# Expert layer's end: gathers after the last tile but one, the last tile's rows by one-hot products

## What is computed

```python
x = _layernorm(x)                                   # 1024 tokens, 512 wide
top1 = argmax(softmax(x @ w_router + b_router))     # one of 8 experts for each token
for e in range(8):
    h = gelu(x @ w1[e] + b1[e])                     # 512 -> 2048
    y = h @ w2[e] + b2[e]                           # 2048 -> 512
    out = out + where(top1 == e, y, 0)
x = x + out
```

## Time and profile before

| | us |
|---|---|
| median of three runs | 1984.2 (1982.53 to 1984.51) |
| the profiled execution | 1984.76 |
| its span | 1982.9 |
| busy: TensorE products | 1884.8 (95%) |
| busy: VectorE, ScalarE, GpSimd | 1132.3, 781.4, 803.7 |

### The profile page before, as it was taken

How to read it: one execution, slowest core, us unless ns; L and a number is a source line. 1 busy time by engine, 2 the same in 40 slices (tenths; PEclk the granted TensorE clock), 3 DMA queues, 4 the chain that set the end, 5 groups by cost and what they waited for, 6 DMA issues and landing times. The chain is left out here.

```text
span 1982.9 us, 41168 instructions
## 1 busy us (share of the span) xinstructions
PE 1884.8 (95%) x17350; PEld 1443.9 (73%) x17350; DVE 1132.3 (57%) x2155; ACT 781.4 (39%) x1300; POOL 803.7 (41%) x641
## 2 busy tenths in 40 slices
PE   7999999999999999999999999779879999999995
PEld 6777777777777677677677676657657787989995
DVE  4536556656556557556556666845665353445554
ACT  3224343444444344344334333531234240455663
POOL 2116777677677667677677664000000000100001
PEclk9999999999999999999999999989889999899998
DMA  6122022122122122122121211020031202899993
GB/s 209 54 91 75 28 76 80 33 76 70 41 78 70 39 81 70 39 76 64 50 76 60 65 39 44 30 68 22 2 132 44 91 1 91 343 377 355 356 361 103
DMA packets 107817, 201.28 MB, mean 102 GB/s; under 512 B 9105, under 2 KB 46417, under 8 KB 102529
## 3 DMA queue, kind: packets, MB, share of 16 engines
q1 hardware_dynamic: 106176, 194.44, 28.9%
q0 software_dynamic: 1472, 4.40, 0.7%
HBM read 184.38 MB, written 14.44 MB: 100 GB/s over the span
## 5 line engine op out<-in xcount | busy, mean ns | idle before, releaser
L303 POOL TENSOR_TENSOR arena<-arena,probT 128x512 f32<-128x512 f32 x392 | 502.1, 1281 | 232.0 <-ACT probT L351 207.8
L456 DVE TENSOR_REDUCE negm<-bank 128x1 f32<-128x512 f32 x512 | 327.0, 686 | 181.5 <-PE bank L651 177.1
L437 DVE TENSOR_TENSOR probT<-bank,arena 128x512 f32<-128x512 f32 (+1 forms) x512 | 291.5, 616 | 212.2 <-PE bank L663 212.2
L351 ACT ACTIVATE probT<-probT 128x1024 f32<-128x1024 f32 x256 | 271.1, 1059 | 230.7 <-DVE probT L437 217.8
L345 ACT ACTIVATE arena<-bank 128x512 f32<-128x512 f32 x128 | 76.4, 597 | 474.0 <-PE bank L626 474.0
L279 POOL TENSOR_TENSOR h_lo<-ctx_raw,h_hi 128x512 fp32r<-128x512 f32 x124 | 161.0, 1299 | 172.6 <-ACT h_hi L328 168.0
L681 PEld LDWEIGHTS bank<-probT,arena 128*32 128x32 f32 x4096 | 104.0, 109 | 93.7 <-ACT probT L351 92.3
L626 PE MATMUL bank<-h_hi,w_hi 128*128 128x512 f32 x512 | 152.7, 420 | 11.2 <-ACT h_hi L328 11.2
L663 PEld LDWEIGHTS bank<-q,k 32*128 32x128 f32 x4096 | 126.0, 186 | 46.5 <-issue 44.2
L626 PE MATMUL bank<-w_hi,h_hi 128*128 128x512 f32 x512 | 152.3, 419 | 0.0
L663 PE MATMUL bank<-q,k 32*128 32x128 f32 x4096 | 150.2, 283 | 0.5 <-DVE probT L437 0.5
(11 more groups left out here) (240 smaller groups left out, 2727.3 us busy)
## 6 DMA issues: line engine op xcount, KB each, us to landing
arena<-w SPq DMA_DIRECT2D x10, 4096.0 KB, 14.5
w_sb<-w SPq DMA_DIRECT2D x40, 1024.0 KB, 6.5
x_res<-bias_table SPq DMA_DIRECT2D x64, 512.0 KB, 5.1
ctx_raw<-ctxT SPq DMA_DIRECT2D x124, 256.0 KB, 3.2
slots<-arena SPq DMA_DIRECT2D x17, 256.0 KB, 3.0
arena<-down SPq DMA_DIRECT2D x11, 256.0 KB, 2.7
b_sb<-b SPq DMA_DIRECT2D x10, 256.0 KB, 6.8
arena<-slots SPq DMA_DIRECT2D x10, 256.0 KB, 9.1
```

What stands on the lines that cost most here:

```text
L303: pool.tensor_tensor(total[:, g], total[:, g], part, ALU.add).then_inc(add_step, 1)
L351: act.activation(pT[:, u % 2, j:j + 2], pT[:, u % 2, j:j + 2], ACT.Exp).then_inc(exp_done, 1)
L437: dve.tensor_tensor(pT[:, u % 2, j, i0:], sc[:, i0:], shift[:, g, j].unsqueeze(1).broadcast_to([P, ST - i0, T]), ALU.add).then_inc(shifted, 1)
L456: dve.tensor_reduce(negm[:, c, h:h + 1], sc[:], AX.X, ALU.max, negate=True).then_inc(max_done, 1)
```

## The change

The gathers wait for the store of tile 8 instead of tile 9, whose y is no longer stored. To tell GpSimd of it, SyncE waits for `y_out[0]` and then loads a small column a second time into `marker`; GpSimd waits for `row_in` to reach 32. The gathered rows of tokens whose slot lies in tile 9 are set to nothing by a multiply with `early` (1 where the slot lies before tile 9), and GpSimd itself adds the rows to `x_res`.

Tile 9's y stays in SBUF. It is split in `y_hi` (ScalarE) and `y_lo` (VectorE). TensorE spreads the slot numbers of the tokens over all partitions (a transpose of a broadcast column, eight times, banks 7 and 0), VectorE compares them with the slot number of each partition's own row of tile 9 (`found_at`, a one-hot matrix for each group), and TensorE multiplies `found_at` of each group with `y_hi` and `y_lo` into a bank. VectorE adds the bank to `x_res`, after GpSimd's add of the group. The routing has five more steps (ROUTED 24 becomes 29), and SyncE has one more small load, `own_row`, at the start of the phase.

```diff
-        MINE, SLOTS, ROUTED = 6, 17, 24
+        MINE, SLOTS, ROUTED = 6, 17, 29
...
+        found_at = h_hi[:, 0:B, :]
+        y_hi, y_lo = [h_lo[:, 4 * i:4 * i + 4, :].rearrange("p j t -> p (j t)") for i in range(2)]
+        out_bank = [1, 2, 3, 4, 5, 1, 2, 3]
-        back_in = [sem(f"e_back_in{b}") for b in range(B)]
+        back_in = [sem(f"e_back_in{i}") for i in range(2)]
```

SyncE:

```diff
+                sp.dma_start(own_row[:], env["own_row_in"]).then_inc(row_in, 16)
                 load_b1(sp, env, 0, 0)
...
                 store(last * 2, 0, y_out[0])
-                store(last * 2 + 1, 1, last_out)
+                sp.wait_ge(y_out[0], last * 16 + 16)
+                sp.dma_start(marker[:], env["own_row_in"]).then_inc(row_in, 16)
```

GpSimd:

```diff
-                pool.wait_ge(last_out, 16)
+                pool.wait_ge(v_step, ROUTED)
+                pool.wait_ge(row_in, 32)
                 for b in range(B):
                     pool.indirect_dma_start(out=back[:, b, :], out_offset=None, in_=env["xs_dram"][:, :],
                                            in_offset=bass.IndirectOffsetOnAxis(ap=slot_u[:, b:b + 1], axis=0)
-                                            ).then_inc(back_in[b], 16)
+                                            ).then_inc(back_in[b // (B // 2)], 16)
+                for b in range(B):
+                    pool.wait_ge(back_in[b // (B // 2)], 16 * (B // 2))
+                    pool.tensor_scalar(back[:, b, :], back[:, b, :], early[:, b:b + 1], None, ALU.mult
+                                       ).then_inc(back_added, 1)
+                    pool.wait_ge(back_added, 2 * b + 1)
+                    pool.tensor_tensor(x_res[:, b, :], x_res[:, b, :], back[:, b, :], ALU.add).then_inc(back_added, 1)
```

ScalarE, behind the loop:

```diff
+                act.wait_ge(y_done, last * 2 + 2)
+                act.activation(y_hi, y[:], ACT.Copy).then_inc(y_hi_done, 1)
```

VectorE, routing:

```diff
+                    step(dve.tensor_copy(slot_k[:], slot_f))
+                    step(dve.tensor_copy(last_slot[:, 0:1], env["last_pair"][:]))
+                    step(dve.tensor_scalar(last_slot[:, 0:1], last_slot[:, 0:1], 2.0 * P, float(P), ALU.mult, ALU.add))
+                    step(dve.tensor_scalar(early[:], slot_k[:], last_slot[:, 0:1], None, ALU.is_lt))
+                    dve.wait_ge(row_in, 16)
+                    step(dve.tensor_tensor(last_slot[:, 1:2], last_slot[:, 0:1], own_row[:], ALU.add))
```

VectorE, behind the loop:

```diff
+                dve.wait_ge(spread_mm, 2)
+                for i, at in enumerate((7, 0)):
+                    dve.tensor_scalar(found_at[:, 4 * i:4 * i + 4, :], bank[at][:].rearrange("p (b t) -> p b t", b=4),
+                                      last_slot[:, 1:2], None, ALU.is_equal).then_inc(found, 1)
+                dve.wait_ge(y_hi_done, 1)
+                dve.tensor_tensor(y_lo, y[:], y_hi.bitcast(F32), ALU.subtract).then_inc(y_lo_done, 1)
                 for b in range(B):
-                    dve.wait_ge(back_in[b], 16)
-                    dve.tensor_tensor(x_res[:, b, :], x_res[:, b, :], back[:, b, :], ALU.add).then_inc(sum_done, 1)
+                    dve.wait_ge(out_mm, b + 1)
+                    dve.wait_ge(back_added, 2 * b + 2)
+                    dve.tensor_tensor(x_res[:, b, :], bank[out_bank[b]][:], x_res[:, b, :], ALU.add).then_inc(sum_done, 1)
```

TensorE, behind the loop:

```diff
+                pe.wait_ge(copied, last * 2 + 3)
+                for i, at in enumerate((7, 0)):
+                    for b in range(4):
+                        mm = pe.transpose(bank[at][:, b * T:(b + 1) * T],
+                                          slot_k[:, 4 * i + b:4 * i + b + 1].broadcast_to([P, P]), ident[:])
+                    mm.then_inc(spread_mm, 1)
+                pe.wait_ge(y_lo_done, 1)
+                for b in range(B):
+                    pe.wait_ge(found, b // 4 + 1)
+                    if b >= 5:
+                        pe.wait_ge(sum_done, b - 4)
+                    for i, part_of in enumerate((y_hi, y_lo)):
+                        mm = pe.matmul(bank[out_bank[b]][:], found_at[:, b, :], part_of, start=(i == 0), stop=(i == 1))
+                    mm.then_inc(out_mm, 1)
```

More of the change, by code:

```diff
@@ L1504, in expert_phase @@
         last_tile = sb("last_tile", [P, 1], I32)
+        slot_k = sb("slot_k", [P, B], F32)
+        last_slot = sb("last_slot", [P, 2], F32)
+        early = sb("early", [P, B], F32)
+        own_row = sb("own_row", [P, 1], F32)
+        marker = sb("marker", [P, 1], F32)
+        found_at = h_hi[:, 0:B, :]
+        y_hi, y_lo = [h_lo[:, 4 * i:4 * i + 4, :].rearrange("p j t -> p (j t)") for i in range(2)]
+        out_bank = [1, 2, 3, 4, 5, 1, 2, 3]
         v_step, ones_set, rank_mm, spot_done, x_out = (sem("f_v_step"), sem("f_ones"), sem("f_rank_mm"),
                                                        sem("f_spot"), sem("f_x_out"))
-        MINE, SLOTS, ROUTED = 6, 17, 24
+        MINE, SLOTS, ROUTED = 6, 17, 29
         back = w1[0].rearrange("p c n -> p (c n)")[:, 0:B * D].rearrange("p (b d) -> p b d", b=B)
@@ L1512, in expert_phase @@
         y_out = [sem(f"e_y_out{i}") for i in range(2)]
-        last_out = sem("e_last_out")
+        spread_mm, found, y_hi_done, y_lo_done, out_mm = (sem("e_spread_mm"), sem("e_found"), sem("e_y_hi"),
+                                                          sem("e_y_lo"), sem("e_out_mm"))
         w2_hi_done, w2_lo_done, h_hi_done, h_lo_done = sem("e_w2_hi"), sem("e_w2_lo"), sem("e_h_hi"), sem("e_h_lo")
@@ L1517, in expert_phase @@
         sum_done, stored = sem("e_sum"), sem("e_stored")
-        back_in = [sem(f"e_back_in{b}") for b in range(B)]
+        back_in = [sem(f"e_back_in{i}") for i in range(2)]
+        back_added, row_in = sem("e_back_added"), sem("e_row_in")
         def last_pair(engine):
@@ L1614, in _ @@
                 tile(1, 1, 0)
-                with act.Fori(1, last_pair(act) + 1) as i:
+                last = last_pair(act)
+                with act.Fori(1, last + 1) as i:
                     for s in range(2):
                         tile(i * 2 + s, s, i)
+                act.wait_ge(y_done, last * 2 + 2)
+                act.activation(y_hi, y[:], ACT.Copy).then_inc(y_hi_done, 1)
             @block.vector
@@ L1703, in _ @@
                     finish(s, s, 0)
-                with dve.Fori(1, last_pair(dve) + 1) as i:
+                last = last_pair(dve)
+                with dve.Fori(1, last + 1) as i:
                     for s in range(2):
@@ L1776, in _ @@
                 tile(1, 1, 0)
-                with pe.Fori(1, last_pair(pe) + 1) as i:
+                last = last_pair(pe)
+                with pe.Fori(1, last + 1) as i:
                     for s in range(2):
                         tile(i * 2 + s, s, i)
+                pe.wait_ge(copied, last * 2 + 3)
[12 more added lines that the diff above has]
+                    mm.then_inc(out_mm, 1)
 def build(nc, ins, out):
@@ L1848, in constants @@
         "iota_in": np.arange(P, dtype=np.float32),
+        "own_row_in": np.arange(P, dtype=np.float32).reshape(P, 1),
         "lower_in": ((np.arange(E)[None, :] < np.arange(E)[:, None]) * P).astype(np.float32).reshape(-1),
```

## The result

| | before | changed |
|---|---|---|
| median of 20 runs each, us | 1982.87 | 1979.93 |
| profiled execution, us | 1984.76 | 1979.20 |
| its span, us | 1982.9 | 1977.4 |
| last down product to the end of the span, us | 20.92 | 18.89 |
| last sum ends, after the last down product, us | 18.52 | 16.43 |

The ratio is 0.9987, with an interval of 0.9981 to 0.9993: about 2.6 us faster, where 7.65 had been forecast. The spans differ by 5.5 us, but 3.0 us of that lie before the first up product (1702.90 before, 1699.92 after), in work that the change doesn't touch; two executions of one program differ by that much. So from here on every kernel is compared by its **tail**, from the end of the last down product to the end of the span. It went from 20.92 (1982.9 less 1961.98) to 18.89 (1977.4 less 1958.51): 2.0 us.

A forecast was written before the change was run, and what follows sets the result against it. TensorE paces the tiles; transfers and issues bound the old tail, TensorE's and VectorE's chain the new. Last sum 1972.85 plus 2.4 us gives span 1975.25, 7.65 under 1982.9: median 1976.6, range 1975.0 to 1980.0.

The forecast's parts named there:

- The sign that the prediction had set for itself: Prediction wrong if GpSimd's pairs exceed 2.4 us, TensorE stands over 0.2 us before the transposes, or a tile gets longer.
- the multiply has none: GpSimd's multiply had no measured row: priced 0.90 us, between a fill at 0.53 and an add at 1.28.
- The bound of the tail: After tile 9: TensorE's products end at 1972.1, later than GpSimd's eight pairs of 2.27 us, ready at 1971.1.
- the third rival: GpSimd's multiply dearer than the add, 1.5 to 2.5 us, or gathers late: next to no gain, about 1983; chance 0.07.
- Contention, charged at nothing: GpSimd beside VectorE's subtractions: no charge; by the skill's rule about 2 us, the sum 1.0 us later.
- The gathers, by the row of 0.96 us: GpSimd's gather issues beside tile 9: not slowed by VectorE's subtractions; 1.30 us apart, eight issued by 1952.8.
- One input at line rate: Skill's rule for GpSimd's multiply: one-input operations run roughly at line rate, favouring the low end, 0.53 us; sum unchanged.
- The start of GpSimd's work: Beside tile 9: GpSimd's gathers start at 1942.7 after tile 8's store and the marker; multiplies start at 1952.9.
- TensorE's and VectorE's new chain: After the last down product at 1961.98: transposes, comparisons, y_lo, sixteen products, sums; last sum ends at 1972.85.
- The half clock that I took: TensorE's sixteen products: 1.2 GHz from the second group on, done at 1972.1; at 2.4 GHz by 1969.3.
- Code behind the loop: Rival: new instructions of TensorE, ScalarE and VectorE after the loop arrive late, costing 2.0 us, giving 1978.6; chance 0.08.
- The start of the phase: own_row load, some 0.4 us, and five routing steps, 1.0 us: covered, so nothing; 1.4 us if the cover were gone.

The follow-up runs named there:

- the run alone: Kernel before with only the own_row load and the five routing steps added, its end untouched: ratio 0.9997, medians 1982.31 and 1982.72 us.

## Why the prediction was wrong

What the change does was forecast rightly: the gathers moved beside tile 9, and the tail became shorter. The size was wrong, and so was what bounds the new tail: TensorE's products were to end last, and GpSimd's pairs did, by far. The sign that the prediction had set for itself, pairs above 2.4 us, came with 2.90. The step that failed is the term "the multiply has none ... the row on its other side is the add of two tensors, 1.28; ... I take the middle, 0.90". The row it was bounded by was no bound: I took it that one tensor read must cost less than two. The same engine does a multiply by a column in 1.57 us and by a constant in 1.49, an add of two tensors in 1.28, and a product with a column read at stride nought in 1.04. Eight times 1.57 less 0.90 is 5.4 us.

Point by point:

- **The bound of the tail.** The pairs came to 2.90 us, where 2.27 stood in the sum, and GpSimd became the bound. What happened is the third rival ("dearer than the add", 1.5 to 2.5 us, within 4 us of before), which had only 0.07; the multiply is at its lower edge. The range of times held the median of 1979.93, which is luck: the kernel before was itself 1.3 us lower over 20 runs than over three. I had put 0.88 on more than 0.2%; it was 0.13%.
- **Contention, charged at nothing.** In the pairs it cost 0.7 us: the first multiply took 1.69 us beside h_lo and the fourth add 1.83 beside y_lo (0.12 + 0.55). The Trainium skill, GPSIMD Engine Reference, section Key points, says that GpSimd shares its SBUF interfaces with VectorE's instructions on two SBUF inputs; the traces agree in kind. By that rule I had priced some 2 us on the pairs, three times what it was. (VectorE had 1.7 us of such work in tile 9 after 1952.9, not the 1.3 that I read.)
- **The gathers, by the row of 0.96 us.** The second and third gather took 1.39 and 1.48 us, 0.9 us more. They ran beside VectorE's subtractions, but so did the next five, in 0.94 to 1.00 us, and in two other executions (the multiply issued twice, and the adds that wait for each other) all eight took 0.94 to 0.99, seven of them beside the same subtractions. So the row was one favourable case, and what decides between the two is open.
- **One input at line rate.** The Trainium skill, GPSIMD Engine Reference, section Engine selection, puts one-input operations roughly at line rate, faster than two-input ones. The trace disagrees for a multiply by a scalar: 1.57 us against 1.28 for the add of two tensors. So the rule that spoke for the low end of my bounds misled here as the row did.
- **The start of GpSimd's work.** From VectorE's write of tile 8's y to the first gather I had 6.15 us, measured 6.23 (1939.30 less 1933.07). The multiplies began 0.8 us later than priced, 0.7 of it between the start of the first gather and the end of the last.
- **TensorE's and VectorE's new chain.** Down product to first of the sixteen products: 3.4 forecast, 2.97 measured. The half clock that I took was not granted in this profile. Of the ten profiles with these products the clock was high throughout in five (3.92 to 3.96 us for sixteen); in the other five it stood at 1.00 through the idle time and fell to 0.50 within the first two microseconds of the products, much as forecast (5.5 us). So it was an even choice, worth 1.6 us in the products, and it matters only where GpSimd isn't the bound.
- **Code behind the loop.** The transposes start at 1958.35, 0.23 after the start of the last down product at 1958.12. ScalarE's y_hi starts 0.03 us after y is written, and VectorE's comparisons 0.04 us after the transposes. No gap on any of the three: the rival of late code fell.
- **The start of the phase.** Nothing, as forecast and as the run alone shows.

The sum with what was measured: GpSimd's chain was 6.5 us longer than priced (0.8 until the first multiply, 5.7 in the pairs, 23.9 for 18.2), less the 1.0 us by which TensorE's chain had been the later one, is 5.5 us; the forecast of 7.65 becomes 2.1, and the tail gained 2.0. Of the 5.7 us in the pairs, 5.0 are the price of an undisturbed pair (2.90 for 2.27, eight times) and 0.7 the contention.

## What to carry to other kernels

When an engine has no row for an operation, a row of a "heavier" operation is not an upper bound: measure the form first, and try the other forms of the same arithmetic (here the broadcast product at 1.04 us beside the scalar multiply at 1.57). Work that is moved off the critical path onto one idle engine should be added up as a chain of its own, from its first start to its last end, and shared with another engine that is idle in the same stretch: ScalarE did the masks at no cost in the tail. Before a stream of two-tensor operations is put on GpSimd beside VectorE's own, look at what VectorE still has to deliver there.

## What the runs showed of the hardware

- GpSimd's float32 128x512, undisturbed: multiply by a column 1.56 to 1.57 us, by a constant 1.49; add of two tensors 1.26 to 1.29; product with a broadcast column 1.04.
- Eight adds of two tensors on GpSimd without a gap held a subtraction of two SBUF tensors on VectorE, begun 0.33 us before them, for 10.79 us, until they had ended (one execution). With a gap of 0.14 us between the adds one subtraction ended per add. In two other kernels a subtraction that began 0.06 us after the first of eight adds without a gap took 1.8 us. A stream of scalar multiplies cost VectorE 0.5 us (beside the first multiply by the constant it was 0.8: w_lo 2.91 for 2.50, h_lo 1.09 for 0.69). Copies and comparisons out of PSUM ran beside either at their usual 0.68 to 0.75 us.
- After 2.0 to 2.6 us of idleness behind short transposes TensorE's products were granted the full clock in five profiles, and in the other five the half clock, from their first or second microsecond on and for some three microseconds.

What stays open: why the scalar form is the slower one on GpSimd, what makes the difference between a subtraction held for one add and for eight, what slows some of the gathers, what decides between the two clocks, and whether GpSimd's adds would also hold out an operation of VectorE that reads one SBUF tensor; the last was not tried, since VectorE has none in that stretch.
